# K of the first batch's last 160 keys among the transposes of x, its scores ahead of V, the bias behind the first attention

## The reference

```python
xn = layernorm(x)
q, k, v = xn @ Wq, ctx @ Wk, ctx @ Wv                       # 16 heads of 64
dots = einsum('bhid,bhjd->bhij', q, k) * 64 ** -0.5
attn = softmax(where(mask[:, None], -finfo.max, dots))
x = x + tanh(g_xattn) * (einsum('bhij,bhjd->bhid', attn, v) @ Wo + bo)
xf = layernorm(x)
idx = argmax(softmax(xf @ Wg + bg))
y = gelu(xf @ W1[idx] + b1[idx]) @ W2[idx] + b2[idx]
out = x + tanh(g_ffn) * y
```

## Time and profile before

| | us |
|---|---|
| median of 3 runs | 207.76 |
| the profiled execution | 207.76 |
| its span | 205.9 |
| TensorE busy | 191.5 (93%) |
| VectorE busy | 125.5 (61%) |
| ScalarE busy | 105.7 (51%) |
| GpSimd busy | 89.5 (43%) |
| mean granted clock of TensorE | 0.989 of full speed |

### The profile page before, as it was taken

How to read it: one execution, slowest core, us unless ns; L and a number is a source line. 1 busy time by engine, 2 the same in 40 slices (tenths; PEclk the granted TensorE clock), 3 DMA queues, 4 the chain that set the end, 5 groups by cost and what they waited for, 6 DMA issues and landing times.

```text
span 205.9 us, 3970 instructions
## 1 busy us (share of the span) xinstructions
PE 191.5 (93%) x1250; PEld 139.1 (68%) x1250; DVE 125.5 (61%) x526; ACT 105.7 (51%) x378; POOL 89.5 (43%) x129
## 2 busy tenths in 40 slices
PE   7899989889999999999999799998999999979960
PEld 7544584656676544788875566774888889869940
DVE  2897675799998322154338999988834347164520
ACT  3232444799999121301427699997641254435510
POOL 7000460576767930000002799677930003777451
PEclk9999999999999999999999999999999999999995
DMA  5995398999999000390000010700000000264111
GB/s 132 347 380 189 99 371 275 338 302 320 289 199 339 22 5 0 95 313 0 3 2 0 26 54 28 207 5 0 0 3 2 0 0 29 86 175 144 33 32 49
DMA packets 21506, 25.17 MB, mean 122 GB/s; under 512 B 1939, under 2 KB 19805, under 8 KB 21344
## 3 DMA queue, kind: packets, MB, share of 16 engines
q1 hardware_dynamic: 19456, 22.51, 36.1%
q0 software_dynamic: 1152, 2.12, 3.1%
q10 hardware_dynamic: 864, 0.15, 0.4%
HBM read 14.14 MB, written 11.68 MB: 125 GB/s over the span
## 4 chain that ended last, share of the span: by engine, by line
PE 80%; DVE 9%; ACT 4%; issue 2%; DMA 1%; POOL 1%; POOLq 0%; DVEq 0%; ACTq 0%
PE s_bank L1610 14%; PE o_bank L1562 13%; PE o_bank L1693 7%; PE s_bank L1650 7%; PE t_bank L1667 7%; PE s_bank L1910 6%; PE o_bank L1921 6%; PE s_bank L1719 4%; PE o_bank L1686 4%; ACT probs L779 3%; PE s_bank L1899 2%; PE t_bank L1701 2%; DVE probs L1250 2%; DMA rows<-in_x_dram 1%; DVE pT L1271 1%
## 5 line engine op out<-in xcount | busy, mean ns | idle before, releaser
L618 POOL TENSOR_TENSOR probs<-probs,r_col 128x512 f32<-128x512 f32 x32 | 33.4, 1043 | 60.6 <-DVE r_col L1261 60.2
L779 ACT ACTIVATE probs<-probs,negm_run 128x160 f32<-128x160 f32 x128 | 53.0, 416 | 6.0 <-DVE negm_run L1250 5.9
L1250 DVE CUSTOM_DVE_ANT_0 probs<-s_bank,maskneg 128x160 f32<-128x160 f32 x128 | 33.2, 318 | 5.8 <-PE s_bank L1650 5.6
L1610 PE MATMUL s_bank<-xnT,wq_sb 128*128 128x512 f32 x64 | 28.8, 598 | 0.5 <-ACT xnT L728 0.5
L1562 PE MATMUL o_bank<-wo_sb,oT 128*128 128x256 f32 x128 | 28.6, 379 | 0.0
L1562 PEld LDWEIGHTS o_bank<-wo_sb,oT 128*128 128x128 f32 x128 | 23.9, 190 | 3.5 <-issue 0.5
L779 ACT ACTIVATION_READ_ACCUMULATOR probs<-probs,negm_run 128x1 f32 x128 | 24.1, 188 | 0.0
L1650 PE MATMUL s_bank<-k_sb,q_sb 64*128 64x160 f32 x256 | 22.3, 311 | 0.0
L1650 PEld LDWEIGHTS s_bank<-k_sb,q_sb 64*128 64x128 f32 x256 | 17.9, 186 | 4.8 <-issue 4.0
L1610 PEld LDWEIGHTS s_bank<-xnT,wq_sb 128*128 128x128 f32 x64 | 11.7, 190 | 13.6 <-issue 13.5
L1667 PE MATMUL t_bank<-ident,probs 128*128 128x128 f32 x128 | 18.7, 284 | 1.3 <-ACT v_sb L801 0.6
(11 more groups left out here) (156 smaller groups left out, 298.6 us busy)
## 6 DMA issues: line engine op xcount, KB each, us to landing
sorted_rows<-empty_row SPq DMA_DIRECT2D x8, 1040.0 KB, 13.5
oT<-in_L_ffn_W_dram SPq DMA_DIRECT2D x1, 2048.0 KB, 18.6
q_sb<-in_L_ffn_W_dram SPq DMA_DIRECT2D x1, 2048.0 KB, 8.3
oT<-sorted_rows SPq DMA_DIRECT2D x1, 1040.0 KB, 5.6
oT<-sorted_rows SPq DMA_DIRECT2D x8, 130.0 KB, 2.3
wq_sb<-in_L_xattn_Wq_dram SPq DMA_DIRECT2D x2, 512.0 KB, 6.1
mask_sb<-in_mask_BxSxS_bk_dram SPq DMA_DIRECT2D x2, 512.0 KB, 7.1
wk_sb<-in_L_xattn_Wk_dram SPq DMA_DIRECT2D x1, 1024.0 KB, 11.0
```

The costliest lines, as they stand in the source:

```text
L618: nc.gpsimd.tensor_tensor(window_wide(u), window_wide(u), r.rearrange("p i h -> p (i h)") .unsqueeze(2).broadcast_to([P, 4, WIDE]), ALU.mu ...
L779: last = nc.scalar.activation(window_part(u, i, h), window_part(u, i, h), ACT.Exp, bias=negm_run[at], scale=-1.0, accum_out=l_run[at])
L1250: nc.vector.tensor_tensor_reduce(window_part(u, i, h), s_bank[u % 2][:, h, i * CK:i * CK + WK], maskneg[:, q, 0:WK], -SCALE, LARGEST, ALU. ...
L1610: last = nc.tensor.matmul(bank[m % 4], wq_sb[:, c, m * P:(m + 1) * P], xnT[:, c, b * N:(b + 1) * N], start=(c == 0), stop=(c == DC - 1))
```

## The change

Of the first batch, the last 160 context rows are now loaded at once, without looking at the mask, on ScalarE's queue, in two loads; behind them on the same queue come the first two quarters of Wk. The other two quarters go on SyncE's queue behind the four tiles of x, ahead of Wq. The two gates are loaded behind ScalarE's last copy of K. TensorE transposes these context rows first, into bank 7, and computes K in four steps between the transposes of x; ScalarE makes all copies of K and of the transposed context. The products of ones at the start are five instead of nine, and two behind the context instead of four between the transposes. The mask's product of the first batch is made behind the block tests, on VectorE. In `attend_window(0)` the first two units' scores go ahead of V, the first two units' exponentials ahead of ScalarE's copy of V, and both sums ahead of VectorE's. The probabilities' transposes wait for ScalarE's first copy of V, and only those that write bank 7 for all copies. GpSimd adds `bo` behind the first batch's last unit. SyncE writes the empty rows when V's first part is done. `find_windows` takes the branch `rest(False)` only if the first batch's window is the last one. In the other branch, which doesn't run here, the waits follow.

```diff
+        LAST = NB - WB
+
+        def wk_cols(u):
+            return slice((u - 1) * 2 * P, u * 2 * P)
+
+        def early_k_bank(u):
+            return bank[6 if u == KU else u]
...
             for q in range(QT):
                 sp.dma_start(x_sb[:, q, :], x[0, q * P:(q + 1) * P, :]).then_inc(s_x_tile[q], 16)
+            for u in range(3, KU + 1):
+                sp.dma_start(wk_sb[:, :, wk_cols(u)], wk.rearrange("(c p) n -> p c n", p=P)[:, :, wk_cols(u)])\
+                    .then_inc(s_wk[u - 1], 16)
             load_wq(0)
...
-            sp.dma_start(wk_sb[:], wk.rearrange("(c p) n -> p c n", p=P)).then_inc(s_wk, 16)
...
             def load_window_ctx():
 
-                for b in range(B):
+                for b in range(1, B):
...
                     if b == 0:
+                        add_bo()
                         pool.wait_ge(s_b2, 16)
...
-            act.dma_start(gate_in[:, 0:1], g_xattn.unsqueeze(0).broadcast_to([P, 1])).then_inc(s_small, 16)
-            act.dma_start(gate_in[:, 1:2], g_ffn.unsqueeze(0).broadcast_to([P, 1])).then_inc(s_small, 16)
+            act.dma_start(ctx_sb[:, 0, 0, :], ctx_in[0, LAST * KB:LAST * KB + WIDE, :]).then_inc(s_early_ctx, 16)
+            act.dma_start(ctx_sb[0:LEFT, 0, 1, :], ctx_in[0, LAST * KB + WIDE:S, :]).then_inc(s_early_ctx, 16)
+            for u in range(1, 3):
+                act.dma_start(wk_sb[:, :, wk_cols(u)], wk.rearrange("(c p) n -> p c n", p=P)[:, :, wk_cols(u)])\
+                    .then_inc(s_wk[u - 1], 16)
...
+            act.wait_ge(early_ctxT_ps, 1)
+            nc.scalar.copy(ctxT[:, :, 0:WK], bank[7].rearrange("p (c k) -> p c k", c=DC)[:, :, 0:WK]).then_inc(early_ctxT, 1)
             for t in range(QT):
                 act.wait_ge(first_var, t + 1)
                 nc.scalar.activation(std[:, t:t + 1], rows[:, t, VAR:VAR + 1], ACT.Sqrt, bias=eps[:]).then_inc(first_std, 1)
+            for u in range(1, KU):
+                take_early_k(u)
             act.wait_ge(pro_ps, 1)
             nc.scalar.copy(xnT[:, 0, 0:N], bank[4]).then_inc(pro_act, 1)
+            take_early_k(KU)
+            act.dma_start(gate_in[:, 0:1], g_xattn.unsqueeze(0).broadcast_to([P, 1])).then_inc(s_small, 16)
+            act.dma_start(gate_in[:, 1:2], g_ffn.unsqueeze(0).broadcast_to([P, 1])).then_inc(s_small, 16)
             act.dma_start(b1_rows, b1).then_inc(s_b1, 16)
...
             any_visible(1)
+            then(nc.vector.tensor_scalar(maskneg[:, :, 0:WK], mask_sb[:, 0:QT, LAST * KB:S], -BIG, None, ALU.mult))
             find_windows()
...
             pe.wait_ge(ident_ready, 2)
-            keep_busy(9)
+            keep_busy(5)
             pe.wait_ge(ident_ready, E + 3)
...
-            xn_transposes(0, (2, 1, 0, 1))
+            early_context()
+            keep_busy(2)
+            pe.wait_ge(early_ctxT, 1)
+            early_keys(1)
+            xn_transpose(0, 0)
+            early_keys(2)
+            xn_transpose(0, 1)
+            xn_transpose(0, 2)
+            early_keys(3)
+            xn_transpose(0, 3)
+            early_keys(4)
             pe.wait_ge(s_wq[0], 16)
...
+                if b == 0 and m == 1:
+                    pe.wait_ge(early_k, KU)
...
+                    else:
+                        pe.wait_ge(first.v_act, b * 2 + 2)
+                        pe.wait_ge(first.v_dve, b * 2 + 2)
...
+                else:
+                    scores(0)
+                    scores(1)
+                    pe.wait_ge(s_wv, 16)
+                    pe.wait_ge(pro_act, 3)
+                    pe.wait_ge(b1_ready, 1)
+                    project_v(0)
                 also("v0")
                 project_v(1)
                 project_v(2)
...
                     if job == 0:
-                        pe.wait_ge(first.v_act, b * 2 + 2)
-                        pe.wait_ge(first.v_dve, b * 2 + 2)
+                        pe.wait_ge(first.v_act, b * 2 + 1)
```

More of the change, by code:

```diff
@@ L68, in __init__ @@
         self.sxT_ready = sem(f"sxT_ready_{name}")
-        self.h_ps = sem(f"h_ps_{name}")
-        self.h_ready = sem(f"h_ready_{name}")
+        if name == "over":
+            self.h_ps = sem(f"h_ps_{name}")
+            self.h_ready = sem(f"h_ready_{name}")
         self.hT_ps = sem(f"hT_ps_{name}")
@@ L262, in flamingo_kernel @@
         s_mask = [sem(f"s_mask{b}") for b in range(B)]
-        s_wk = sem("s_wk")
+        s_wk = [sem(f"s_wk{u}") for u in range(1, KU + 1)]
+        s_early_ctx = sem("s_early_ctx")
+        early_ctxT_ps = sem("early_ctxT_ps")
+        early_ctxT = sem("early_ctxT")
+        early_k_ps = sem("early_k_ps")
+        early_k = sem("early_k")
         s_wv = sem("s_wv")
@@ L481, in rest @@
                 sp.wait_ge(empty_ready, 2)
-                sp.wait_ge(first.k_ps, KU)
+                if later_too:
+                    sp.wait_ge(first.k_ps, KU)
+                else:
+                    sp.wait_ge(first.v_ps, 1)
                 for k in range(CH):
@@ L790, in attend_window @@
             def attend_window(b, fill, also):
[L791 to L794, removed]
+                if b > 0:
+                    for u in range(0, KU, 2):
+                        act.wait_ge(first.k_ps, (b - 1) * KU + (u + 1))
+                        nc.scalar.copy(*window_k_dst(u + 1)).then_inc(first.k_act, 1)
+                        also(f"k{u}")
+                else:
+                    for u in range(2):
+                        window_exp(b, u)
                 act.wait_ge(first.v_ps, b * 3 + 1)
                 nc.scalar.copy(*window_v_dst(0)).then_inc(first.v_act, 1)
-                for u in range(2):
-                    window_exp(b, u)
+                if b > 0:
+                    for u in range(2):
+                        window_exp(b, u)
                 act.wait_ge(first.v_ps, b * 3 + 3)
@@ L1467, in rest @@
                     else:
-                        w = dve.value_load(window[0:1, b:b + 1], min_val=0, max_val=NB - WB)
+                        w = LAST if b == 0 else dve.value_load(window[0:1, b:b + 1], min_val=0, max_val=NB - WB)
                         attend_window(b, w, next_q if b == 0 else first_rows_drain,
@@ L1526, in _, with xn_transpose, early_context, early_keys @@
             pe.wait_ge(ident_ready, 2)
-            keep_busy(9)
+            keep_busy(5)
             pe.wait_ge(ident_ready, E + 3)
-            def xn_transposes(b, between=(0,) * QT):
-                for i in range(QT):
-                    pe.wait_ge(ln_ready, b * QT + i + 1)
-                    for c in range(DC):
-                        last = nc.tensor.transpose(bank[4 + c][:, i * P:(i + 1) * P],
-                                                   xn[:, b * QT + i, c * P:(c + 1) * P], ident[:])
-                        if i == QT - 1:
-                            last.then_inc(pro_ps, 1)
-                    keep_busy(between[i])
+            def xn_transpose(b, i):
+                pe.wait_ge(ln_ready, b * QT + i + 1)
+                for c in range(DC):
+                    last = nc.tensor.transpose(bank[4 + c][:, i * P:(i + 1) * P],
+                                               xn[:, b * QT + i, c * P:(c + 1) * P], ident[:])
+                    if i == QT - 1:
+                        last.then_inc(pro_ps, 1)
+            def early_context():
+                pe.wait_ge(s_early_ctx, 32)
+                for c in range(DC):
+                    nc.tensor.transpose(bank[7][:, c * CK:c * CK + WIDE], ctx_sb[:, 0, 0, c * P:(c + 1) * P], ident[:])
+                    last = nc.tensor.transpose(bank[7][:, c * CK + WIDE:c * CK + WK], ctx_sb[0:LEFT, 0, 1, c * P:(c + 1) * P],
+                                               ident[0:LEFT, 0:LEFT])
+                last.then_inc(early_ctxT_ps, 1)
+            def early_keys(u):
+                pe.wait_ge(s_wk[u - 1], 16)
+                for i in range(2):
+                    m = 2 * u - 2 + i
+                    for c in range(DC):
+                        last = nc.tensor.matmul(early_k_bank(u)[:, i * CK:i * CK + WK], wk_sb[:, c, m * P:(m + 1) * P],
+                                                ctxT[:, c, 0:WK], start=(c == 0), stop=(c == DC - 1))
+                last.then_inc(early_k_ps, 1)
             def visit_sums():
@@ L1972, in rest @@
             def rest(later_too):
-                xn_transposes(1)
+                for i in range(QT):
+                    xn_transpose(1, i)
                 if later_too:
                     context(first, 0, 0)
-                else:
-                    window_context(0)
                 for b in range(B):
```

90 lines of the change are left out of this document (49 added, 41 removed).

## The result

| | before | after |
|---|---|---|
| median | 207.73 us (207.56 to 207.84, 4 runs) | 206.10 us (205.84 to 206.43, 4 runs) |
| ratio | | 0.9927, 95% interval 0.9914 to 0.9940 |
| profiled execution, its span | 207.76, 205.9 | 205.88, 204.1 |

The change makes the kernel faster by 1.6 us, where 3.9 were forecast. The sign is right and the time lies in the range, near its upper end (206.2), but 2.3 us of the forecast gain are missing. The profile shows that of the two terms of the sum one was right (the gain behind the transposes) and the other (the shift of Q) was off by 2.3 us.

The account below looks back on a forecast made before the run. TensorE's path was taken to bound the kernel, except where it waited behind the first two units' exponentials and sums. A 6.9 us gain less Q starting 3.0 us later gave 3.9 us: 207.76 to 203.9 us, range 203.2 to 206.2.

Parts of the forecast that it names:

- the gain behind the transposes: From the second batch's x transposes' end to the third unit's maxima: 7.0 us instead of 13.9, 6.9 us sooner.
- the shift of Q: At the kernel's start, Q begins at 12.3 us instead of 9.31 because K precedes it: 3.0 us later.
- Step 1, the context load: At the start, both context pieces, issued first on ScalarE's queue, land at 4.3 us.
- Step 2 and 3: Before K, context transposes at the lower clock take 1.2 us, to 5.5; two products of ones then lead to 6.45.
- K's slices stand ahead of Wq and land sooner still: Loads at the start: K's weights land before Wq's first half, itself forecast at 11.1 us, in time for 12.3.
- Step 4: K 4.58 us and eight x transposes 0.88, plus 0.2 for the low clock in the first slice; K ends at 12.1.
- the clock rises late: Rival at K: one to three slices at 1.2 GHz, 1.1 us more each, 204.8 to 207.0 us; chance 0.20.
- Hand-overs: Between K's end at 12.1 us and Q's start at 12.3: 0.2 us allowed.
- The norms, Wq, the masks, the bias rows: Inputs for Q, block tests and the stretch behind the fifth head slip but stay covered; no added time counted.
- The rival by which the transfers come last: At the start, loads up to Wq's first half delay Q to 13.3 us, total 204.9 us; chance 0.06.
- The sentence on the queue rule: At the start, interleaved queues could delay the last norm by 1.9 us instead of 1.6; K would still cover it.
- The forecast's case: Whole kernel at 203.2 to 204.8 us, around the forecast 203.9; chance 0.60.

Follow-up runs that it names:

- the split quarter with five ones: Changed kernel with Wk's first quarter loaded in two halves, one on each queue, five products of ones kept at the start; 204.69 us, ratio 0.9856.
- the kernel with six ones and the split quarter: Changed kernel with Wk's first quarter loaded in halves on two queues and six products of ones at the start, not five; 203.43 us, repeated 204.81.

## Why the prediction was off

Point by point, in the order of the prediction:

- *What bounds the kernel.* Right. TensorE's path and the exponentials of the first two units decided; the gain behind the transposes was 6.95 us (13.91 less 6.96) where the sum had 6.9, and it was kept through the loop. That it needs the scores ahead of V was right in sign, but I priced this part at 0.8 us (0.9 in the sum) and it is 2.5 by time less Q: the wait for ScalarE's copy of x, 1.31 us, is missing in that working, and the rest was 1.1. It was in the total all the same, since the stretch of the earlier trace rows that I subtracted from starts at the transposes.
- *Step 1, the context load.* 4.3 us forecast, 4.02 measured: 0.3 better.
- *Step 2 and 3, the context transposes and two ones at the low clock.* 1.2 and 0.95 us forecast, 1.26 (4.02 to 5.28) and 1.22 measured: 0.3 worse.
- *"K's slices stand ahead of Wq and land sooner still."* This is the first step that failed. I costed the quarters by their place in the queue relative to Wq, and never set a landing time for the first of them against 6.45. It landed at 6.9 and K's first matmul came at 7.07: 0.6 us. The rows that I had pointed to it: x tiles issued at 0.8 to 2.2 took 2.9 us with a single queue, and the quarter was issued at 1.7 with 256 KB of its own and another queue beside it. The wait varies from execution to execution (0.25 to 0.74 us in the four profiles with the same instructions up to Q).
- *Step 4, "0.2 more is for the part of the first slice before the clock rises".* This is the term that was mis-sized most. K and the x transposes take 7.55 us (7.07 to 14.62) instead of 5.66: 1.9 us. I took the moment of the rise from the kernel before, where nine ones and no load stood ahead of it. It was the first rival, "the clock rises late", to which I gave 0.20; its price of 1.1 us for each slow step fits (1.12 and 0.82), and its range, 204.8 to 207.0, holds the measured 206.10. Its worst case had 0.5 us for the eight x transposes at the low clock; a pair takes 0.43 us there against 0.22, so it should have been 0.8.
- *Hand-overs.* 0.2 forecast, none seen.

Together 3.0 - 0.3 + 0.3 + 0.6 + 1.9 - 0.2 = 5.3 us, the measured shift. 6.95 - 5.3 - 0.15, the last for Q and the transposes behind it, is the 1.5 us by which the values come sooner.

- *The norms, Wq, the masks, the bias rows.* All covered, as said. The rival by which the transfers come last didn't come true either; the 1.6 us for landing in its price stand in no row. The block tests end at 21.45 in the changed kernel and are asked for at 22.51.
- *The bias addition.* Nothing, as said; the run with it back shows the same time.
- *The sentence on the queue rule.* I used it for the x tiles alone, which K covered, and not for K's own quarter. By the Trainium skill ("DMA: Bandwidth & Descriptors", "Issuing engines are not separate DMA queues") loads issued by different engines run on the same sixteen DMA engines and interleave. The trace agrees: with the second queue beside them x's tiles took a median of 3.6 us to land instead of 2.9.
- *The forecast's case had 0.60.* The pause before the context and the missing ones were named as speaking for the rival, and the reason given against it ("isn't solid now either") was not worked out from any row. The likeliest single value should have been that of one or two slow steps.

So the step that failed is the fourth one: K was priced at full clock, with 0.2 us for the time before the rise, and the low clock cost 1.9 us more. Beside it the landing of K's first quarter, put at nothing, cost 0.6. The sign was right for the reason given: the shift was 5.3 us, and 5.9 in the kernel's second profile (Q at 15.22), both below the 6.9 that would use up the gain. That the time lies in the range is owed to the range's upper end, which allowed for two slow slices, and not to the forecast's own case.

What stays open: what sets the moment of the rise in one execution rather than another, and why the same load on the same queue lands at 6.2 us in one and 7.6 in the next. The runs show both, with the same program. The wait for Wk alone doesn't set the rise: with the load in time the clock was late (the split quarter with five ones), with a wait of 0.98 us it was early (six ones and three), and with K starting at 7.07 and 7.08 it rose near 11.6 in one execution and near 9.1 in the other. Whether a wait delays the rise in part can't be told from them.

The loads' profile rows behind the 3.6 us, then the block tests' end:

```profile
rows<-in_x_dram SPq DMA_DIRECT2D x4, 128.0 KB, 3.6
```

```profile
21.26 0.19 DVE L1063 TENSOR_TENSOR visit_p<-fullb,blockmin 128x32 f32<-128x32 f32 x1
```

## What to carry to other kernels

Work moved to the very start of a kernel isn't moved at its old price: look at the duration of weight loads there (here 333 ns against 190), and try keeping TensorE at work up to the moved instructions (ratio 0.9850 with six ones ahead of the context and three behind it, 0.9940 with none, in the same rounds). One execution isn't enough to judge such a start: the same program had Q at 14.62 and 15.22. For a load at the head of the queues, set its own landing time against the moment it is wanted, instead of comparing it with loads behind it. And when a block is taken out from between two others, list the waits that it hid: here the copy of a bank, 1.3 us, which only the new order of the scores covered.

## What the runs showed of the hardware

- A pause of 1.35 us (6.5 to 7.9) was followed by a granted clock of 0.50 for more than 3 us in the middle of dense matmuls (nine ones). After a pause of 0.98 us in another execution the clock stayed up (six ones and three).
- At the low level one step of K (eight instructions of 160 columns) takes 2.13 to 2.27 us where it takes 1.09 to 1.19 at the high one, so it is about the full factor of two; a pair of x transposes 0.43 against 0.22. The weight loads take 333 to 337 ns where the granted clock reads 0.50, and 190 at the high level.
- The column of the granted clock reads 1.00 at the start of every profile, also where weight loads take 333 ns, and it doesn't show the first rise (near 11.6 us in the changed kernel). It fell below 1.00 in these starts only where the clock went down again after a rise (0.85, 0.50, 0.94 in the rows above). For the first microseconds the durations are to be believed.
- The same instructions up to Q started Q at 13.43, 13.68, 14.62 and 15.22 us in four executions, and in the kernel with six ones and the split quarter at 11.6 and 15.9.
- VectorE's mask product for the first batch took 3.44 us beside GpSimd's bias addition, and 0.48 us in the changed kernel, where GpSimd did nothing at that time.
